# A vision tower on one core: the token mixing of the last attention made by VectorE instead of GpSimd

## What is computed

```
normed = _ln(hidden_states, g1, b1)
scores = jax.nn.sigmoid(jnp.einsum('bld,d->bl', normed, Wr) + br)
_, idx = jax.lax.top_k(-scores, k)          # k = 4 of 26 tokens
attn_mask = jnp.zeros((b, l), bool).at[jnp.arange(b)[:, None], idx].set(True)
...
attn_out = ctx @ Wo + bo
w = scores / (jnp.sum(scores, axis=1, keepdims=True) + 1e-06)
pooled = jnp.einsum('bl,bld->bd', w, normed)
mix_out = (normed + scores[..., None] * pooled[:, None, :]) @ Wm + bm
merged = jnp.where(attn_mask[..., None], attn_out, mix_out)
h = hidden_states + merged
```

## Time and profile before

| | us |
|---|---|
| median of 3 runs | 3202.85 |
| lowest and highest | 3193.87, 3208.3 |
| the profiled execution's own time | 3200.74 |
| its span | 3198.9 |
| the mixed attention's turns 1 and 2, 3009.3 to 3041.4 and 3041.4 to 3072.6 | 32.1, 31.2 |

### The profile page before, as it was taken

One profiled execution on the slowest core, in us unless ns is written; L12 is line 12 of the kernel. 1 busy time (PEld: TensorE's weight loads), 2 busy tenths in 40 slices (PEclk: granted clock), 3 DMA queues, 4 the chain that ended last, 5 costly groups with the idle time before them and its releaser, 6 DMA issues. The chain is left out here.

```text
span 3198.9 us, 56413 instructions
## 1 busy us (share of the span) xinstructions
PE 2882.0 (90%) x19833; PEld 2667.6 (83%) x19833; DVE 2136.1 (67%) x5307; ACT 1087.1 (34%) x2206; POOL 649.6 (20%) x768
## 2 busy tenths in 40 slices
PE   7979999999999999999977997896979889876877
PEld 6769999999999999999977887674768779766767
DVE  3857777767777777767776766234467567777776
ACT  2433333323333333323324333213435233334423
POOL 1311212121121212121121100112223112122440
PEclk8979999999999999999998999798979879988888
DMA  3010000000000000000010000560000010000000
GB/s 132 8 46 36 18 35 35 35 35 18 35 35 35 18 35 35 35 35 18 18 37 1 2 2 6 158 203 30 1 11 19 7 46 18 11 1 15 23 18 17
DMA packets 24032, 105.58 MB, mean 33 GB/s; under 512 B 4407, under 2 KB 9415, under 8 KB 18526
## 3 DMA queue, kind: packets, MB, share of 16 engines
q1 hardware_dynamic: 22222, 99.62, 9.0%
q0 software_dynamic: 1584, 3.30, 0.3%
HBM read 98.32 MB, written 6.64 MB: 33 GB/s over the span
## 5 line engine op out<-in xcount | busy, mean ns | idle before, releaser
L820 ACT ACTIVATE hid<-bank,dat 128x384 f32<-128x384 f32 (+1 forms) x912 | 555.1, 609 | 1149.3 <-PE bank L535 1033.9
L787 PE MATMUL bank<-w,hid_hi 128*128 128x384 f32 x2964 | 858.1, 361 | 2.2 <-DVE y_tok L834 1.6
L789 PE MATMUL bank<-w,hid_lo 128*128 128x192 f32 x2964 | 745.8, 252 | 0.0
L789 PEld LDWEIGHTS bank<-w,hid_lo 128*128 128x128 f32 x2964 | 571.0, 193 | 1.8
L787 PEld LDWEIGHTS bank<-w,hid_hi 128*128 128x128 f32 x2964 | 561.6, 189 | 5.8 <-issue 4.1
L852 DVE TENSOR_TENSOR hid_lo<-hid,hid_hi 128x384 fp32r<-128x384 f32 (+1 forms) x912 | 540.0, 592 | 31.5
L849 DVE CAST hid_hi<-hid 128x384 fp32r<-128x384 f32 (+1 forms) x912 | 341.4, 374 | 133.7 <-ACT hid L820 130.3
L863 DVE SCALAR_TENSOR_TENSOR h_tok<-bank,gate,h_tok 128x192 f32<-128x192 f32 x416 | 173.6, 417 | 249.7 <-PE bank L789 245.3
L535 PE MATMUL bank<-xa_hi,w_hi 128*128 128x384 f32 (+1 forms) x912 | 326.5, 358 | 8.6 <-DVEq L2181 8.6
L535 PE MATMUL bank<-xa_hi,w_lo 128*128 128x384 f32 (+1 forms) x912 | 323.0, 354 | 0.0
L535 PE MATMUL bank<-xb,w_hi 128*128 128x384 f32 (+1 forms) x912 | 322.7, 354 | 0.0
(11 more groups left out here) (357 smaller groups left out, 4540.9 us busy)
## 6 DMA issues: line engine op xcount, KB each, us to landing
raw<-in_L_exp SPq DMA_DIRECT2D x36, 1344.0 KB, 5.8
w_e<-in_L_exp SPq DMA_DIRECT2D x20, 576.0 KB, 3.9
w_e<-in_L_exp SPq DMA_DIRECT2D x20, 384.0 KB
pix<-in_pixels SPq DMA_DIRECT2D x6, 832.0 KB, 10.8
w_e<-in_L_exp SPq DMA_DIRECT2D x20, 195.0 KB
raw<-in_L_mlp SPq DMA_DIRECT2D x2, 1344.0 KB, 5.7
wp_raw<-in_L_att SPq DMA_DIRECT2D x1, 2304.0 KB, 8.9
route_rows<-in_rows_clear SPq DMA_DIRECT2D x1, 2000.0 KB, 22.6
```

The source lines that it names most:

```text
L787: nc.tensor.matmul(o[:, 0:2 * D], hid_hi[k % 2][:, m, c], w2[j][:, m, :], start=m == 0, stop=False)
L789: ins = nc.tensor.matmul(o[:, 0:D], hid_lo[k % 2][:, m, c], w2[j][:, m, 0:D], start=False, stop=m == HC - 1)
L820: nc.scalar.activation(hid[(6 * k + m) % 3][:, 0:128 * nt], bank[4 + (6 * k + m) % 4][:, 0:128 * nt], func, bias=bias).then_inc(s["h_act"] ...
```

## The change

GpSimd's `mixing` goes, with six semaphores. `pool_images` makes the shares, the pooled rows, the raise and the addition one behind the other on VectorE, at the place where it made the pooled rows. A new `mask_mixed` makes the keeping on VectorE at the start of `split_result`. Each step is chained to the next by VectorE's own semaphore (`route_link`). VectorE now waits for `s_all` and `m_all` itself. GpSimd keeps `blocks` and `stage`. The arithmetic stays as it was.

```diff
--- before.py
+++ after.py
@@ -231,8 +231,7 @@
                  ("rows_clear", "tables", "counted", "ranked", "slots", "places", "rows_out", "x_turned", "x_kept", "up_full",
                   "hid_full", "h_turned", "h_kept", "y_full", "y_kept", "b_full", "b_used", "step")}
         mix = {n: ctx.enter_context(nc.semaphore("mix_" + n)) for n in
-               ("early", "factors", "logits", "scores", "s_out", "s_in", "s_all", "ranked", "m_out", "m_all", "shares",
-                "pooled", "raised", "added", "kept", "mixed", "step")}
+               ("early", "factors", "logits", "scores", "s_out", "s_in", "s_all", "ranked", "m_out", "m_all", "step")}
         factors = {n: ctx.enter_context(nc.semaphore("factors_" + n)) for n in ("in", "out_in", "full", "moved")}
         wide_in = {n: ctx.enter_context(nc.semaphore("wide_" + n)) for n in
                    ("qkv", "out", "high", "low", "out_high", "out_ready")}
@@ -1422,39 +1421,6 @@
             def by_images(x):
                 return x.rearrange("p (m t) -> p m t", t=SLOT)
 
-            def mixing(pool, i, step):
-
-                ti = slice(n * i, n * i + n)
-                both = [128, 2, n]
-                if step == "shares":
-                    if i == 0:
-                        pool.wait_ge(mix["s_all"], 16)
-                    nc.gpsimd.tensor_tensor(shares, of_turn(feat, i), s_b[:, ti].unsqueeze(1).to_broadcast(both),
-                                            ALU.mult).then_inc(mix["shares"], 1)
-                    pool.wait_ge(mix["shares"], i + 1)
-                elif step == "raise":
-                    pool.wait_ge(mix["pooled"], i + 1)
-                    for c in range(2):
-                        ins = nc.gpsimd.tensor_tensor(
-                            by_images(shares[:, c, :]), by_images(s_b[:, ti]),
-                            pooled[:, c, 16 * i:16 * i + 16].unsqueeze(2).to_broadcast([128, 16, SLOT]), ALU.mult)
-                    ins.then_inc(mix["raised"], 1)
-                    pool.wait_ge(mix["raised"], i + 1)
-                elif step == "add":
-                    nc.gpsimd.tensor_tensor(of_turn(feat, i), of_turn(feat, i), shares, ALU.add).then_inc(mix["added"], 1)
-                    pool.wait_ge(mix["added"], i + 1)
-                else:
-                    if i == 0:
-                        pool.wait_ge(mix["m_all"], 16)
-                    nc.gpsimd.tensor_copy(mask_row[:, ti], mask_b[0:1, ti])
-                    nc.gpsimd.tensor_scalar(shares[:, 0, :], mask_b[:, ti], -1.0, 1.0, ALU.mult, ALU.add)\
-                        .then_inc(mix["kept"], 1)
-                    pool.wait_ge(mix["kept"], i + 1)
-                    nc.gpsimd.tensor_tensor(of_turn(feat, i), of_turn(feat, i),
-                                            shares[:, 0, :].unsqueeze(1).to_broadcast(both), ALU.mult)\
-                        .then_inc(mix["mixed"], 1)
-                    pool.wait_ge(mix["mixed"], i + 1)
-
             def gpsimd(pool):
                 nc.gpsimd.memset(n_tok[:, :, :], 0.0).then_inc(s["bd_zero"].sem, 1)
                 if rel_kind:
@@ -1492,14 +1458,6 @@
                     blocks(t)
                     if t < 14:
                         stage(t + 2)
-                    if cfg.mix:
-                        i, g = divmod(t, G)
-                        if g == 0 and i:
-                            mixing(pool, i - 1, "keep")
-                        elif g:
-                            mixing(pool, i, ("shares", "raise", "add")[g - 1])
-                if cfg.mix:
-                    mixing(pool, NI - 1, "keep")
 
 
             ready = s["att_ready"].at
@@ -1871,16 +1829,34 @@
                     nc.vector.tensor_scalar(m26, m26, KEEP - 0.5, None, ALU.is_lt).then_inc(mix["ranked"], 1)
 
                 def pool_images(i):
-                    mc = slice(16 * i, 16 * i + 16)
-                    dve.wait_ge(mix["shares"], i + 1)
-                    route_link(nc.vector.tensor_reduce(total, by_images(s_b[:, n * i:n * i + n]), AX.X, ALU.add))
-                    route_link(nc.vector.tensor_scalar(total, total, 1e-6, None, ALU.add))
+
+                    mc, ti = slice(16 * i, 16 * i + 16), slice(n * i, n * i + n)
+                    if i == 0:
+                        dve.wait_ge(mix["s_all"], 16)
+                    route_link(nc.vector.tensor_tensor(shares, of_turn(feat, i),
+                                                       s_b[:, ti].unsqueeze(1).to_broadcast([128, 2, n]), ALU.mult))
                     nc.vector.tensor_reduce(pooled[:, :, mc], shares.rearrange("p c (m t) -> p c m t", t=SLOT),
                                             AX.X, ALU.add)
+                    route_link(nc.vector.tensor_reduce(total, by_images(s_b[:, ti]), AX.X, ALU.add))
+                    route_link(nc.vector.tensor_scalar(total, total, 1e-6, None, ALU.add))
                     route_link(nc.vector.reciprocal(total, total))
-                    nc.vector.tensor_tensor(pooled[:, :, mc], pooled[:, :, mc],
-                                            total.unsqueeze(1).to_broadcast([128, 2, 16]), ALU.mult)\
-                        .then_inc(mix["pooled"], 1)
+                    route_link(nc.vector.tensor_tensor(pooled[:, :, mc], pooled[:, :, mc],
+                                                       total.unsqueeze(1).to_broadcast([128, 2, 16]), ALU.mult))
+                    for c in range(2):
+                        ins = nc.vector.tensor_tensor(
+                            by_images(shares[:, c, :]), by_images(s_b[:, ti]),
+                            pooled[:, c, mc].unsqueeze(2).to_broadcast([128, 16, SLOT]), ALU.mult)
+                    route_link(ins)
+                    route_link(nc.vector.tensor_tensor(of_turn(feat, i), of_turn(feat, i), shares, ALU.add))
+
+                def mask_mixed(i):
+                    ti = slice(n * i, n * i + n)
+                    if i == 0:
+                        dve.wait_ge(mix["m_all"], 16)
+                    nc.vector.tensor_copy(mask_row[:, ti], mask_b[0:1, ti])
+                    route_link(nc.vector.tensor_scalar(shares[:, 0, :], mask_b[:, ti], -1.0, 1.0, ALU.mult, ALU.add))
+                    route_link(nc.vector.tensor_tensor(of_turn(feat, i), of_turn(feat, i),
+                                                       shares[:, 0, :].unsqueeze(1).to_broadcast([128, 2, n]), ALU.mult))
 
                 if cfg.mix:
                     factors()
@@ -2052,7 +2028,7 @@
                         dve.wait_ge(s["job_used"].sem, b["job_used"] + at["out", i - 1, 1] + 1)
                     dve.wait_ge(s["av_used"].sem, b["av_used"] + halves * G * (i + 1))
                     if cfg.mix:
-                        dve.wait_ge(mix["mixed"], i + 1)
+                        mask_mixed(i)
                         of3 = o_f[:, 0:2 * n].rearrange("p (c n) -> p c n", c=2)
                         link(nc.vector.tensor_tensor(of3, of3, mask_b[:, n * i:n * i + n].unsqueeze(1)
                                                      .to_broadcast([128, 2, n]), ALU.mult))
```

## The result

The changed kernel takes 3209.16 us in the median of 16 runs (3203.76 to 3216.26), the kernel before 3199.37 us beside it (16 runs, 3191.86 to 3208.3). The ratio is 1.0033, with a 95% interval of 1.0023 to 1.0043: 9.8 us slower, within 0.5%.

The account below looks back on a forecast made before the run. A turn was taken as bound by VectorE's 19.7 us from waited shift to spread plus TensorE's 12.3. Terms of 7.85 us plus 3.5 for the clock gave +11.3, forecast 3213 us; range 3205 to 3221, with part rivals 3201 to 3223.

Parts of the forecast that it names:

- The loop: A mixed turn is 19.7 us on VectorE, shift to spread, then 12.3 us on TensorE: 32 us together.
- Splits, +0.15 each: Splits 0 to 2: 1.8 us of mask work added, 1.65 us of stretched L2068 gone; +0.45 us in all.
- the third rival: SBUF port: GpSimd's copies and casts block VectorE's two-input instructions, up to 14 us in all, 3227 us; chance 0.12.
- Pooling 0, +0.7; 1 and 2, +2.15 each: Pooling adds 3.35 us a turn, less 1.18 of spread's stretch; the first also loses a 1.49 us wait.
- The end, +0.6 and +1.8: Behind pooling 3, GpSimd's later copies delay the last values by 0.6 us; split 3 costs TensorE its full 1.8 us.
- The clock, +3.5: Longer TensorE idle time ahead of the scores brings slow 1.2 GHz stretches of nearly 8, 8 and 7.3 us: +3.5 us.
- The first: Rival: VectorE's 5.35 us of gaps a turn take the new work; 3193 us, or 3189; chance 0.06.
- The second: Rival: behind each spread TensorE stays at 1.2 GHz up to VectorE's next wait, +20 us, 3230 us; chance 0.08.

Follow-up runs that it names:

- the ballast: Changed kernel plus three more 128x832 products on VectorE: ahead of spread, turns of 36.1, 38.3, 37.9 us; behind group 0's normalisation, 32.7, 35.0, 34.6 us.
- the fillings of six and of four products: Identity products on TensorE ahead of its wait for spread: six in the changed kernel, 1.0016 times before; four in the kernel before, 0.9983.

## Why the prediction was right

The direction, the size and the class came out: 11.3 us forecast, 9.8 measured over the runs, 8.8 between the spans of the two profiled executions, 10.2 in M. The mechanism, VectorE's stretch from the waited shift to `spread`, was right. That the total is so close is in part luck, since the clock term was too large where it was put and nothing was put where it was missing. By its own steps:

- **The loop.** Right, and shown by the ballast: what stands between the waited shift and `spread` counts in full, what stands behind the normalisation of group 0 costs at most 0.1 us a turn.
- **Splits, +0.15 each.** From the first new instruction to the next shift it takes 6.90 us, where the split took 6.71: +0.2. The stretch of 1.65 us paid for 1.8 us of keeping. That both products take 1.15 us is the third rival at a small scale, 0.3 us a turn.
- **Pooling 0, +0.7; 1 and 2, +2.15 each.** In the first, the end of `spread` moved by 0.3 us against the first shift, less than forecast, since in that turn the small instructions of the pooled rows took 2.37 us before, not the 2.13 of the next (2986.34 to 2988.71, 3018.69 to 3020.82), and `spread` came down by 1.25. The price itself was met: 5.47 us from the shares to `spread` for 2.13, +3.34. In the middle turns split and pooling together moved VectorE's part from 19.7 to 22.0 us: +2.3, as the sum has it.
- **The end, +0.6 and +1.8.** Too small. From the last shift of that kind, 3069.92 and 3074.72, o_lo is done 28.4 and 31.7 us later: +3.3. The last split has its 1.8. What failed is the +0.6, the slack of the last values: it took GpSimd's copies for what sets their start and TensorE's work ahead of them for as long as before. The last values start 1.5 us later against that shift, and not 0.75 (split and slack together), and GpSimd's copies are done 0.7 us before that (3094.57 + 0.95, the values at 3096.25). TensorE's own chain sets them. Behind a wait of 1.89 us for ScalarE, which was there before too, the second half of turn 2's projection ran at 1.2 GHz for 2.9 us, 0.55 us an instruction, and before at the full clock, 0.35 us. First the kernel before:

```profile
3084.06 0.45 PE L535 MATMUL bank<-o_hi,wp_hi 128*128 128x416 f32 x1 [1.89 <-ACT v_x L1745]
3084.35 0.35 PE L535 MATMUL bank<-o_lo,wp_hi 128*128 128x416 f32 x1
```

  and the changed one:

```profile
3089.07 0.71 PE L534 MATMUL bank<-o_hi,wp_hi 128*128 128x416 f32 x1 [1.89 <-ACT v_x L1703]
3089.58 0.55 PE L534 MATMUL bank<-o_lo,wp_hi 128*128 128x416 f32 x1
```

  From that projection's start to the last values but one it takes 8.6 us for 7.3, +1.3. At the full clock the copies would have set the start after all, about 0.7 us earlier, so that about half of it is the slow clock's own. Why the clock fell there in one kernel and not in the other is not shown.
- **The clock, +3.5.** The mechanism holds, and the fillings of six and of four products show it as a cost of its own. The size was wrong by place. In the turns it was put too large: TensorE's part of them changed by -0.05, +0.5 and +1.1 us, 1.5 in all, since the slow stretches lasted 6.4, 6.5 and 5.8 us and not 8. The difference of the two fillings in the turns, 8.8 less 6.7, gives 2.1. At the end it was put at nothing, and there the slow projection of turn 2 and the last one (11.06 us from o_lo to the first addition for 10.46, at 1.2 GHz to its end) make +1.3 and +0.6. The trend from idle time to the length of the slow stretch, drawn through four rows, was no law: the same 5.04 us gave 6.5 and 5.8, and the 8.0 us of the earlier trace rows went on to 8.6.
- **The rivals.** The first is refuted. The second did not occur where it was placed, behind `spread`; but slow stretches longer than its 11 us are real, 12.6 us at the end of this kernel, and with the keeping alone on VectorE 15.3 us behind a wait of 3.25. The third was there at 0.3 us a turn; mostly GpSimd waited, as argued. By the Trainium skill (SBUF — State Buffer, Who interferes with whom) the port pair that the two engines share is an exclusive lock, and the order of issue decides which of them is blocked. By that rule the trace agrees in both directions: GpSimd's block copies take 1.91 us for 0.95 beside VectorE's products, and with the keeping alone on VectorE L2071, begun 0.3 us behind GpSimd's shares, takes 2.25 us for 0.59 and ends 0.45 us behind them.

## What to carry to other kernels

Before moving work between engines, find the stretch of the receiving engine that another engine waits on, and the stretch in which the receiving engine waits: the same seven instructions cost 10 us in the first and gave 8 us against the kernel before in the second. An engine "beside the path" may not be beside it: work on GpSimd was stretching VectorE's path by 2.8 us a turn, about as much as doing the pooling there costs. And an idle time of TensorE is paid twice, as itself and in the slow clock behind it, so a filling that fits into the wait is worth a try. One that overruns it gives back part or all of the gain, and where there is no wait it costs its whole length.

## What the runs showed of the hardware

Two things I had not expected. Filling a wait with products of the identity gave 4.4 to 9.9 us of a phase of 140 (5.4 us of the whole, on either kernel), and nothing where eleven overran it; the very same six products cost 10.7 us of M where the wait had gone. And the slow stretch behind a wait has no fixed length: 5.04 us of idle time were followed by 6.5 and by 5.8 us at 1.2 GHz, 3.25 us by 15.3 us, 1.28 us (TensorE ahead of the same projection in the kernel before) by none. The same 1.89 us were followed by none in the kernel before and by 2.9 us in the changed one, and the same 5.46 us by 8.6 us in the kernel before and by 3.5 us in the run with the pooling alone.
